# A fused four-layer attention and feed-forward kernel: one step of the second attention re-sorted on VectorE, and TensorE's products of the second and third attention re-sorted

## The reference

```python
def attention2(xn, ctx):                # 32 batches of 64 queries and 64 keys, causal
    q, k, v = xn @ Wq.T + bq, ctx @ Wk.T + bk, ctx @ Wv.T + bv       # 16 heads of 8
    s = einsum('bhtd,bhsd->bhts', q, k) / sqrt(8) + causal
    return einsum('bhts,bhsd->bhtd', softmax(s), v).reshape(...) @ Wo.T + bo

x = x + attention2(layernorm(x), ctx)
x = x + ffn2(layernorm(x))              # 8 and 16 bit rounding, 128 -> 512 -> 128
x = x + attention3(layernorm(x), ctx)   # as above with a band added to the scores, and a top-k cut
x = x + ffn3(layernorm(x))              # 8 experts, the best two of each token
```

## Time and profile before

| | |
|---|---|
| median of 3 runs | 845.35 us (844.32 to 845.65) |
| the profiled execution | 847.62 us |
| its span | 845.5 us |
| PE busy | 808.1 us (96% of the span) |
| DVE busy | 629.2 us (74%) |
| ACT busy | 563.5 us (67%) |
| POOL busy | 286.7 us (34%) |
| scores of the second attention (L1986) | 601.8 to 676.4 us |
| scores of the third attention (L1986) | 722.2 to 804.8 us |

### The profile page before, as it was taken

The page is one execution under the profiler, slowest core; times in us unless marked ns, Lnnn a source line. Parts: engine busy times, 40 slices in busy tenths (PEclk is TensorE's granted clock), DMA queues, the critical chain, the costliest instruction groups (busy, mean ns, idle before and its releaser), DMA issues.

```text
span 845.5 us, 20299 instructions
## 1 busy us (share of the span) xinstructions
PE 808.1 (96%) x7358; PEld 565.8 (67%) x7358; DVE 629.2 (74%) x1586; ACT 563.5 (67%) x1598; POOL 286.7 (34%) x587
## 2 busy tenths in 40 slices
PE   8999999999999999899999999999899989999986
PEld 8887888999998987554444444444467665676652
DVE  5678777777777665766875967765989867899866
ACT  3666667777777776796455576456478779778744
POOL 4246444454444335200000000002147520345445
PEclk9999999999999999999999999999999999999999
DMA  8700000000000000000000000000000000000000
GB/s 336 170 3 1 1 1 2 1 2 1 1 2 2 2 1 2 1 1 0 1 0 1 1 1 0 1 0 1 1 28 3 3 3 1 3 3 3 16 15 26
DMA packets 7886, 13.54 MB, mean 16 GB/s; under 512 B 4342, under 2 KB 5100, under 8 KB 7532
## 3 DMA queue, kind: packets, MB, share of 16 engines
q1 hardware_dynamic: 7788, 12.24, 4.6%
HBM read 11.19 MB, written 1.05 MB: 14 GB/s over the span
## 4 chain that ended last, share of the span: by engine, by line
PE 68%; DVE 13%; ACT 8%; issue 5%; POOL 4%; DMA 1%; DVEq 0%; POOLq 0%; SPq 0%; ACTq 0%
PE psum L1561 10%; PE psum L772 7%; PE psum L812 6%; PE psum L840 6%; PE psum L755 5%; PE psum L764 3%; ACT arena L910 2%; PE psum L2016 2%; PE psum L1547 2%; PE psum L1570 2%; PE psum L2523 2%; DVE arena L2120 2%; PE psum L2401 2%; PE psum L1986 2%; PE psum L829 2%
## 5 line engine op out<-in xcount | busy, mean ns | idle before, releaser
L517 POOL TENSOR_TENSOR ve<-mv,epsv 128x1 f32<-128x1 f32 x176 | 35.7, 203 | 420.9 <-DVE mv L512 420.9
L1561 PE MATMUL psum<-arena,w1f 128*128 128x512 f32 x240 | 109.5, 592 | 0.0
L520 POOL TENSOR_TENSOR rstd<-ve,epsv 128x1 f32<-128x1 f32 x176 | 101.3, 575 | 13.8
L910 ACT ACTIVATE arena<-psum,negmax 128x128 f32<-128x128 f32 x256 | 90.6, 407 | 22.1 <-DVE negmax L1010 22.1
L1561 PEld LDWEIGHTS psum<-arena,w1f 128*128 128x128 f32 x240 | 45.5, 190 | 48.7 <-issue 44.3
L1100 POOL TENSOR_TENSOR arena<-arena,rsum 128x512 f32<-128x512 f32 x64 | 65.7, 1047 | 24.6 <-DVE rsum L1016 24.6
L1010 DVE TENSOR_REDUCE negmax<-psum 128x8 f32<-128x1024 f32 x32 | 39.2, 1225 | 32.9 <-PE psum L812 32.9
L910 ACT ACTIVATION_READ_ACCUMULATOR arena<-psum,negmax 128x1 f32 x256 | 63.3, 247 | 0.0
L755 PE MATMUL psum<-arena,sclA 128*128 128x128 f32 x512 | 62.5, 275 | 0.1
L772 PE MATMUL psum<-arena 128*128 128x512 f32 x128 | 61.5, 599 | 0.9 <-DVE arena L1005 0.6
L755 PEld LDWEIGHTS psum<-arena,sclA 128*128 128x128 f32 x512 | 59.7, 192 | 0.3 <-ACT arena L964 0.3
(11 more groups left out here) (375 smaller groups left out, 1970.9 us busy)
## 6 DMA issues: line engine op xcount, KB each, us to landing
w<-in_w0qk SPq DMA_DIRECT2D x2, 512.0 KB, 5.0
w<-in_w0vo SPq DMA_DIRECT2D x1, 1024.0 KB, 7.6
cT<-in_cT SPq DMA_DIRECT2D x1, 1024.0 KB, 16.2
out<-x_tok SPq DMA_DIRECT2D x4, 256.0 KB, 2.2
rows<-in_rows SPq DMA_DIRECT2D x1, 836.0 KB, 13.5
x_tok<-in_x_tok SPq DMA_DIRECT2D x1, 768.0 KB, 9.8
ctx_tok<-in_ctx_tok SPq DMA_DIRECT2D x1, 768.0 KB, 11.1
wa<-in_wa SPq DMA_DIRECT2D x1, 768.0 KB, 17.8
```

What stands on the lines that cost most here:

```text
L520: pool.tensor_tensor(rstd[:, u, self.i:self.i + 1], ve[:, u, self.i:self.i + 1], epsv[:, 1:2], ALU.pow) \
L910: m = nc.scalar.activation(e0[:, b, g, :], ps(k, P, j * P), ACT.Exp, bias=negmax0[:, b, g:g + 1], accum_out=sum0[:, b, g:g + 1])
L1561: nc.tensor.matmul(ps(k), w1("e2", j * 384 + arg * D, j * 384 + (arg + 1) * D), f1_Hm[:, n, 2 * j + i, :], start=False, stop=False)
```

## The change

It reorders three tables and mends the cut of one.

- `ATT_PE` (second attention): `v` ahead of `lnt` instead of behind it; `av` at the end of the step, behind `qk` and `lnt0`, instead of between `out` and `qk`.
- `ATT_DVE` (second attention): `tail` behind `s`, the subtraction, instead of ahead of `add`.
- `LATE_PE` (third attention): `lnt` ahead of `av` instead of behind it.
- `drained` cuts at the first kind of the last part in the order, whichever that is, so that the lists of the last part stay what they were.

```diff
-        ATT_PE = [("s", 4), ("lnt", 9), ("v", 5), ("ot", 7), ("t", 5), ("out", 7), ("av", 6), ("qk", 2), ("lnt0", 1)]
+        ATT_PE = [("s", 4), ("v", 5), ("lnt", 9), ("ot", 7), ("t", 5), ("out", 7), ("qk", 2), ("lnt0", 1), ("av", 6)]
...
-        ATT_DVE = [("own", 0), ("max", 4), ("tail", 8), ("add", 7), ("s", 4), ("apply", 0), ("rsum", 6), ("stats", 7), ("av", 6)]
+        ATT_DVE = [("own", 0), ("max", 4), ("add", 7), ("s", 4), ("tail", 8), ("apply", 0), ("rsum", 6), ("stats", 7), ("av", 6)]
...
-            at = order.index(rest[0])
+            at = min(order.index(x) for x in rest)
...
-        LATE_PE = [("f3 gate", 0), ("s", 5), ("qk", 4), ("ot", 7), ("t", 6), ("out", 7), ("f3 p", 0), ("f2 out", 2), ("f2 turn", 3), ("av", 6),
-                   ("lnt", 8)]
+        LATE_PE = [("f3 gate", 0), ("s", 5), ("qk", 4), ("ot", 7), ("t", 6), ("out", 7), ("f3 p", 0), ("f2 out", 2), ("f2 turn", 3),
+                   ("lnt", 8), ("av", 6)]
```

## The result

| | before | after |
|---|---|---|
| median | 845.14 us (4 runs in this comparison) | 857.7 us (855.1 to 858.19, 4 runs) |
| ratio, 95% interval | | 1.0144 (1.013 to 1.0158) |
| profiled execution | 847.62 us | 858.15 us |
| its span | 845.5 us | 856.2 us |

The direction was right; the size was not. I forecast 853.1 and drew the range to 857.0.

The account below looks back on a forecast made before the run. The prediction took two nearly equal loops, the PE-DVE chain and PE's own work, to bound the second attention. Waits of +4.7 there and +3.0 in the third attention made +7.7, so 853.1 us from 845.35, range 847 to 857.

Parts of the forecast that it names:

- Rival 2: Both attentions: only changes of shape hold PE up, so the edit gains 2.4 us, giving 843.0; chance 0.09.
- The rule of the Trainium skill: On PE: changing the tiling mode makes TensorE drain, so by that alone fewer changes are a gain.
- Its own readers (`lnt` in the next step, POOL's bias) come late enough. I cost it at nothing.: Second attention, DVE: `tail` behind the subtraction delays what follows by some 0.3, covered by 0.36 idle, so costs nothing.
- 8 x 0.43 = 3.4: Second attention: eight full steps grow from 4.70 to 5.13 us, 0.43 each.
- +4.7: Second attention in all: the eight full steps plus the early and last ones cost 4.7 us.
- 2.87: Second attention, PE: `out` waits for ACT's `ot` and starts 2.87 us behind `s` instead of 2.72.
- 6 x 0.38 = 2.3: Third attention: in six steps `lnt` waits for ACT to store bank 7, 0.38 us each.
- +0.7: Third attention, behind the last scores: `av` now stands between `lnt` and L2516, costing 0.7 us.
- That execution is 2.3 over the median of the runs, so I forecast 845.35 + 7.7: Whole kernel: the 7.7 us sum is added to the median of the runs, not the profiled execution, giving 853.1.
- rival 4: Whole kernel: the clock also falls to half in three stretches, together 5 us more, giving 858; chance 0.04.
- the +11.4 of the upper bound: Whole kernel: 0.1 more at each of three hand-overs in ten steps and one in seven, giving 856.8.

Follow-up runs that it names:

- e2: The kernel before with only PE's `v` moved ahead of `lnt` in the second attention; 845.6 us, ratio 1.0018.
- e3: The kernel before with only PE's `av` moved behind `lnt0`, to the end of the step, in the second attention; 848.36 us, ratio 1.0042.
- e1: The kernel before with only DVE's `tail` moved behind the subtraction in the second attention; 845.69 us, ratio 1.0007.
- e6: The changed kernel with `qk` of the second attention in bank 5 and `lnt0` in bank 4; 867.32 us, ratio 1.0244 against before.
- e9: The kernel of e6 with DVE's two L526 moved to the end of its step; 856.19 us, ratio 1.0116 against before.
- e4: The kernel before with only `lnt` moved ahead of `av` in the third attention; 851.13 us, ratio 1.0066.
- e7: The changed kernel with ACT also doing `v` ahead of `lnt`, and the bank moves of e6; 862.58 us, ratio 1.0198 against before.
- e8: The changed kernel with twelve unread products on PE ahead of the third attention's `lnt` of tile 12; 855.79 us, ratio 1.0119 against before.
- e12: The kernel of e4 with `lnt` of every tile in bank 6; 848.15 us, ratio 1.0033 against before.
- e10: The kernel before with PE's `lnt` moved behind `lnt0`, to the end of the step, in the second attention; 844.26 us, ratio 0.9979.
- e11: The kernel of e10 with eight unread products ahead of the third attention's `lnt` of tile 12; 842.88 us, ratio 0.9971 against before.

## Why the prediction was wrong in size

**Right.** Both waits of the second attention and their sizes by themselves: `v` +0.18 a step in e2 (I had 0.15), `av` +0.28 in e3 (0.28). The steps of the third attention with `f2 turn`: `lnt` waits 0.37 for ACT, and starts 0.64 behind `f2 turn`, as worked out. Rival 2, the faster one, put PE's changes of shape first. Its condition, bank 7 free within 0.39, was not met: `qk` started 0.84 behind `out`. The rule of the Trainium skill beside it ("TensorEngine Tiling (Array Packing)", Key Properties) is borne out in direction by PE's rows: from `lnt` to the next group it took 0.26 before, to `v` (639.24 - 638.98), and 0.17 after the change, to `ot`, which has its own shape (646.71 - 646.54). That 0.09 is smaller than the waits.

**The steps that failed**, in the prediction's order:

1. *"Its own readers (`lnt` in the next step, POOL's bias) come late enough. I cost it at nothing."* In the steps nearly so, +0.03. But behind the last subtraction PE's `lnt` comes at once and waits 1.78 for the L526. The first `add` there is 0.78 later than in the execution before, as in e1 (0.77). In the table above it does not show, because the execution before had its half-speed stretch at 719 to 723 and the one after had none. That stretch is worth 1.3 to 1.4: e1 has it and ends the part at +0.72, the changed kernel has not and ends it at -0.59.
2. *"8 x 0.43 = 3.4" and the steps around it, +4.7.* Measured +5.65. The eight full steps gave 4.15: six 0.48 to 0.50, one 0.83, and one 0.39, where the execution before has a step of 4.81. Where I had 2.87 from `s` to `out`, it took 2.93: from ACT's end (647.95) to PE's `out` (648.09) 0.14, where I took 0.05, and `v` 1.00 behind `s` instead of 0.94; ACT's `v` followed its store of `lnt` 0.08 sooner than I had. `v` uses bank 6 and waits for DVE's L2143 to read `av` from it (645.83 + 0.27 = 646.10). It does so in e2 too, where `av` has not moved, and not in most steps of e3: it is `v`'s own move that brings it there so early. I had looked at what `v` delays, not at whether its bank is free. In the longer step DVE pauses 0.21 ahead of an L507, without a releaser in the profile, L2143 comes 0.35 later than in the other steps, and `v` waits 0.33 for it. The last three steps gave 1.1 instead of 0.6, the two early ones 0.4 instead of 0.7.
3. *"6 x 0.38 = 2.3."* Measured +3.2. Seven steps lost time where I had six, 0.15 to 0.69, 2.9 together. In the step shown `s` came 1.58 - 1.13 = 0.45 later, since `lnt` to `av` took 0.26 where I had put 0.20. The step of tile 5, costed at nothing, lost 0.29. What made that one longer is L526 beside POOL's L620; that reading is by analogy with e6 and e9. *"+0.7"* behind the last scores was +1.0 in e4.
4. *"That execution is 2.3 over the median of the runs, so I forecast 845.35 + 7.7", and rival 4, the clock, at 0.04.* This step took the result out of the range. The profiled executions differ by 858.15 - 847.62 = 10.5, which is less than the +11.4 of the upper bound, and 845.35 + 10.5 = 855.9 lies inside the range. But the changed kernel's profiled execution is only 0.4 over its median, so the median rose by more. I looked for falls of the clock in the second attention's short pauses, of which none came. The fall came behind the last scores, where my own sum made the longest idle stretch. In the profiled executions it nearly cancels: before had two of 3.4 us (719 and 811), after one of 6.8. Of 26 runs of the kernel before, taken beside e3 and e4, 22 have a mean granted clock of 0.996 to 0.999 and lie at 843.3 to 846.4; three of the four after have 0.994 to 0.995 and lie at 857.3 to 858.2, the fourth has 0.998 and 855.1. That the median is so near rival 4's 858 is luck: that rival had three falls in another place.

The account of the executions closes. Order: 7.7 + 0.95 (second attention) + 0.8 (behind it) + 0.9 (third) + 0.3 (behind the last scores) = 10.65. Clock: before lost 1.35 at 719 and 1.7 at 811 (e3, without that fall, is 1.7 shorter there), after lost 3.2 (e7, with the same order there and no fall, is 3.2 shorter), so +0.15. Less the 0.1 at the start that makes 10.7, the difference of the spans. The forecast of the median was 4.6 too low: 2.8 of that is 10.5 - 7.7, the other 1.8 is the step from execution to median. That this 1.8 is the clock's is supported by e8, whose median is 1.9 lower, and not shown run by run.

Left open: why the clock falls near 720 in one execution and not in another with the same order there (before and e2 fell, e4 and e12 did not), and what the pauses without a releaser are: 0.21 on DVE in the longer step (most executions have one or two longer steps, e2 and e6 none), and 0.6 to 1.1 in PE's `av` behind the last subtraction.

## What to carry to other kernels

When a product moves past another, ask both ways: what does the group that moves up now wait for (its bank, its reader's order), and which wait did the group that moves down cover. Here a change of shape was worth 0.09, and the uncovered wait cost 0.28; e10 found a place where the engine was waiting anyway, and that gained. A cover is worth something only where it exists: follow a "free" move to the end of the loop, and look at what the longest idle stretch that you add does to the clock, and in how many of the runs it is there already. And before you read 0.3 us out of two single executions, see how far executions of the same order lie apart at that place.

## What the runs showed of the hardware

- L526 on DVE (a scale and shift from SBUF to SBUF, 128x128 fp32) lasts 0.34 by itself and until just behind the end of a large instruction of POOL when it starts beside it: 1.13 beside L2159 (1.04), 0.60 beside L620 (0.46). One already well under way was not held up: after the change the second L526 starts at 650.18, lasts 0.34, and L2159 follows at 650.39. The reciprocal that follows in the same step, which reads PSUM, lasted 0.26 beside L2159. The Trainium skill, "GPSIMD Engine Reference", Key points, says that POOL shares its SBUF interfaces with VectorE, in contention with some forms of DVE's instructions. The rows of e6 and e9 agree, and in e6 the price is nearly the whole of POOL's instruction. L526 reads one tensor from SBUF, so of the forms that the page names only the one with a 2-port mode could apply; no run shows which mode it ran in.
- From the end of ACT's L2078 to the start of PE's L2022, which waited for it, it was 0.14, after the change and in e2 and e9 alike.
- Behind the last scores an idle stretch of 1.82 on PE was followed by 6.8 us at the lower clock, by 3.4 or by none, and one of 1.10 by 3.4 or by none, from one execution to another (the counts stand under e8); with that time filled by products nobody reads, the stretch had full clock (e8, e11).
- The half-speed stretch of 3.4 us at 719 was worth 1.35, and that at 811 1.7, by executions with and without them.
